# LayerNorm statistics of two batches in one instruction, over interleaved elements

## The reference

```
def layernorm(x):                       # no scale, no shift
    return (x - mean(x)) / sqrt(var(x) + 1e-5)

# layer 1: cross attention, 16 heads of 16 features, context of 128 x 128 x 256
q      = layernorm(x) @ Wq + bq
k, v   = split(ctx @ Wkv + bkv)
scores = q k^T / 4
attn   = softmax(scores, axis=query)    # over the queries, not the keys
x1     = x + (attn v) @ Wo + bo

# layer 2: a router picks 96 of 128 tokens of each batch
y      = layernorm(x1)
keep   = top_k(y @ w_router, 96)
out    = x1 + where(keep, gelu(y @ w_block), y)
```

## Time and profile before

| | |
|---|---|
| median of 3 runs | 921.36 us (921.07 to 921.6) |
| the profiled execution, span from first to last instruction | 919.4 us |
| around the span, median minus span | 2.0 us |
| PE, ACT, DVE, POOL busy | 889.4, 879.5, 873.5, 796.8 us |
| DVE: statistics of layer 1 (L746), of layer 2 (L735) | 128 x 411 ns, 128 x 414 ns |
| DVE: aggregation of layer 1 (L751), of layer 2 (L740) | 128 x 173 ns, 128 x 160 ns |
| granted clock of PE over the span | 0.994 of full speed |

### The profile page before, as it was taken

How to read it: one execution, slowest core, us unless ns; L and a number is a source line. 1 busy time by engine, 2 the same in 40 slices (tenths; PEclk the granted TensorE clock), 3 DMA queues, 4 the chain that set the end, 5 groups by cost and what they waited for, 6 DMA issues and landing times. The chain is left out here.

```text
span 919.4 us, 31003 instructions
## 1 busy us (share of the span) xinstructions
PE 889.4 (97%) x10306; PEld 753.9 (82%) x10306; DVE 873.5 (95%) x2320; ACT 879.5 (96%) x4503; POOL 796.8 (87%) x1488
## 2 busy tenths in 40 slices
PE   7899999999999999999999999999999999999973
PEld 6788888888888888888888888888888888888861
DVE  6899999999999999999999999999999999999887
ACT  5999999999999999999999999999999999999983
POOL 4568789999989999899999999999899999998865
PEclk9999999999999999999999999999999999999997
DMA  6222123223223223223223223223223222221102
GB/s 198 62 65 71 46 61 95 57 84 93 57 84 95 60 83 92 58 86 91 70 75 91 59 86 91 71 74 89 76 71 89 76 71 87 76 61 53 49 24 92
DMA packets 70976, 70.45 MB, mean 77 GB/s; under 512 B 12064, under 2 KB 62752, under 8 KB 70816
## 3 DMA queue, kind: packets, MB, share of 16 engines
q1 hardware_dynamic: 69456, 67.68, 25.5%
q10 hardware_dynamic: 1360, 0.79, 0.3%
HBM read 35.13 MB, written 16.78 MB: 56 GB/s over the span
## 5 line engine op out<-in xcount | busy, mean ns | idle before, releaser
L567 ACT ACTIVATE e_sb<-ps_s,neg_max 128x128 f32<-128x128 f32 x2048 | 719.1, 411 | 4.4 <-DVE neg_max L712 3.9
L567 ACT ACTIVATION_READ_ACCUMULATOR e_sb<-ps_s,neg_max 128x1 f32 x2048 | 513.5, 251 | 0.0
L712 DVE TENSOR_REDUCE neg_max<-ps_s 128x4 f32<-128x512 f32 x512 | 329.0, 663 | 26.4 <-PE ps_s L337 26.4
L337 PE MATMUL ps_s<-q_eo,k_sb 32*128 32x256 f32 x2048 | 146.6, 400 | 1.1 <-DVE k_sb L790 0.5
L402 PE MATMUL ps_a<-e_sb,v_pad 128*32 128x128 f32 x4096 | 138.4, 276 | 2.2 <-DVE x_sb L729 1.6
L299 PE MATMUL ps_a<-w_o_sb,o_sb 128*128 128x256 f32 x512 | 133.2, 382 | 2.0 <-DVE v_sb L803 1.9
L299 PE MATMUL ps_t<-w_z_sb,xt_sb 128*128 128x258 f32 x512 | 132.6, 381 | 1.3 <-DVE z_sb L815 1.3
L1042 POOL TENSOR_TENSOR v_pad<-v_sb,recip 128x256 f32<-128x256 f32 x128 | 79.6, 622 | 54.0 <-DVE recip L757 52.5
L402 PEld LDWEIGHTS ps_a<-e_sb,v_pad 128*32 128x32 f32 x4096 | 104.1, 109 | 24.0 <-issue 21.6
L337 PEld LDWEIGHTS ps_s<-q_eo,k_sb 32*128 32x128 f32 x2048 | 92.5, 184 | 29.4 <-ACT e_sb L567 17.0
L1031 POOL TENSOR_TENSOR x_sb<-x_sb,bo_sb 128x256 f32<-128x256 f32 x128 | 114.0, 892 | 0.2
(11 more groups left out here) (102 smaller groups left out, 2197.6 us busy)
## 6 DMA issues: line engine op xcount, KB each, us to landing
x_sb<-in_x SPq DMA_DIRECT2D x64, 256.0 KB, 2.9
c_sb<-in_ctx SPq DMA_DIRECT2D x64, 256.0 KB, 3.1
out<-z_sb SPq DMA_DIRECT2D x64, 256.0 KB, 2.4
q_eo<-q_raw SPq DMA_DIRECT2D x504, 32.0 KB, 2.0
z_sb<-in_L_xattn_Wkv ACTq DMA_DIRECT2D x2, 256.0 KB, 7.2
z_sb<-in_L_xattn_Wq ACTq DMA_DIRECT2D x1, 256.0 KB, 4.5
w_z_sb<-in_L_ffn_w_block SPq DMA_DIRECT2D x1, 256.0 KB, 7.6
w_o_sb<-in_L_xattn_Wo SPq DMA_DIRECT2D x1, 256.0 KB, 7.0
```

The source lines that it names most:

```text
L337: mm = nc.tensor.matmul(ps_s[:, bank(b, j), c, :, :], k_sb[rows, r2, c, h * T:(h + 1) * T], q_eo[rows, r2, :, c, h, :], start=True, stop=True)
L567: last = nc.scalar.activation(e_sb[:, b % 4, j, c, par, :], ps_s[:, bank(b, j), c, par, :], ACT.Exp, bias=neg_max[:, b % 4, h:h + 1], accu ...
L712: nc.vector.tensor_reduce(neg_max[:, b % 4, :].rearrange("p (c j q) -> p j c q", c=C, j=J)[:, j, :, :], ps_s[:, bank(b, j), :, :, :], AX.X ...
```

## The change

Two rows of `x_sb` (or `x1_sb`) that lie 256 elements apart are read by one `bn_stats` as 512 elements, the first element of one batch, the first of the other, the second of one, and so on. The even places are then one batch and the odd places the other, so the six numbers that come out are count, mean and sum of squares of either batch, and no aggregation is needed. The epsilon step on POOL multiplies the sum of squares by 1/256 and adds epsilon in the same instruction. The calls go to every second step: the pair of layer 1 to the start of the odd steps, two steps earlier than the aggregation of its second batch stood before; the pair of layer 2 to the end of the odd steps. The last two batches keep statistics and aggregation of their own in layer 2.

```diff
-        st1 = sb("st1", [P, 4, 6])
-        mv1 = sb("mv1", [P, R, 2])
+        st1 = sb("st1", [P, R // 2, 6])
...
+        count_mean_m2 = "p g (q k) -> p (g q) k"
+        mean1 = st1[:, :, :].rearrange(count_mean_m2, q=2)[:, :, 1]
+        m2_1 = st1[:, :, :].rearrange(count_mean_m2, q=2)[:, :, 2]
...
-            def stats2(b):
-                if has(b):
-                    dve.wait_ge(x1_ready, upto(b))
-                    nc.vector.bn_stats(st2[:, b % 4, :], x1_sb[:, b % R, :]).then_inc(st2_ready, 1)
...
+            def stats2_of_pair(b):
+
+                if b % 2 == 0 and has(b):
+                    dve.wait_ge(x1_ready, upto(b + 1))
+                    nc.vector.bn_stats(st2[:, pair(b), :],
+                                       x1_sb[:, b % R:b % R + 2, :].rearrange("p q e -> p e q")).then_inc(st2_ready, 2)
...
-            def aggregate1(b):
-                if has(b):
-                    dve.wait_ge(st1_ready, upto(b))
-                    nc.vector.bn_aggr(mv1[:, b % R, :], st1[:, b % 4, :]).then_inc(mv1_ready, 1)
...
+            def stats1_of_pair(b):
+
+                if b % 2 == 0 and has(b):
+                    dve.wait_ge(x_in[pair(b)], landed(b))
+                    nc.vector.bn_stats(st1[:, pair(b), :],
+                                       x_sb[:, b % R:b % R + 2, :].rearrange("p q e -> p e q")).then_inc(st1_ready, 2)
...
                 if s >= 4:
-                    stats1(s + 10)
-                aggregate2(s - 3)
+                    stats1_of_pair(s + 10 if s == 4 else s + 11)
...
-                stats2(s - 2)
+                stats2_of_pair(s - 3)
...
-            stats2(B - 2)
-            aggregate2(B - 2)
+            stats2_of_one(B - 2)
+            aggregate2_of_one(B - 2)
...
-                    pool.wait_ge(mv1_ready, upto(b + 1))
-                    nc.gpsimd.tensor_tensor(ve1[:, r], mv1[:, r, 1], eps_sb[:, :], ALU.add).then_inc(ve1_ready, 2)
-                    nc.gpsimd.tensor_scalar(neg_m1[:, r], mv1[:, r, 0], -1.0, None, ALU.mult)
+                    pool.wait_ge(st1_ready, upto(b + 1))
+                    nc.gpsimd.tensor_scalar(ve1[:, r], m2_1[:, r], 1.0 / E, EPS, ALU.mult, ALU.add).then_inc(ve1_ready, 2)
+                    nc.gpsimd.tensor_scalar(neg_m1[:, r], mean1[:, r], -1.0, None, ALU.mult)
```

More of the change, by code:

```diff
@@ L81, in cross_attention_routed_ffn @@
         minus_mean = sb("minus_mean", [P, P])
-        eps_sb = sb("eps_sb", [P, 2])
         minus_half = sb("minus_half", [P, 2])
@@ L90, in cross_attention_routed_ffn @@
         rstd1 = sb("rstd1", [P, R])
-        st2 = sb("st2", [P, 4, 6])
-        mv2 = sb("mv2", [P, R, 2])
+        st2 = sb("st2", [P, R // 2, 6])
+        st2_one = sb("st2_one", [P, 2, 6])
         ve2 = sb("ve2", [P, R])
@@ L104, in cross_attention_routed_ffn @@
         beta = sb("beta", [P, 2, GROUP])
+        count_mean_m2 = "p g (q k) -> p (g q) k"
+        mean1 = st1[:, :, :].rearrange(count_mean_m2, q=2)[:, :, 1]
+        m2_1 = st1[:, :, :].rearrange(count_mean_m2, q=2)[:, :, 2]
+        mean2 = st2[:, :, :].rearrange(count_mean_m2, q=2)[:, :, 1]
+        m2_2 = st2[:, :, :].rearrange(count_mean_m2, q=2)[:, :, 2]
+        mean_var_one = st2[:, :, :].rearrange(count_mean_m2, q=2)[:, :, 1:3]
         raw = z_sb[:, :, :].rearrange("p b e -> p (b e)")
@@ L157, in cross_attention_routed_ffn @@
         w_mean_mm, w_z_ready = sem("w_mean_mm"), sem("w_z_ready")
-        st1_ready, mv1_ready, ve1_ready, rstd1_ready = sem("st1_r"), sem("mv1_r"), sem("ve1_r"), sem("rstd1_r")
-        st2_ready, mv2_ready, ve2_ready, rstd2_ready = sem("st2_r"), sem("mv2_r"), sem("ve2_r"), sem("rstd2_r")
+        st1_ready, ve1_ready, rstd1_ready = sem("st1_r"), sem("ve1_r"), sem("rstd1_r")
+        st2_ready, ve2_ready, rstd2_ready = sem("st2_r"), sem("ve2_r"), sem("rstd2_r")
+        st2_one_ready, mean_var_one_ready = sem("st2_one_r"), sem("mean_var_one_r")
         xhat_ready = sem("xhat_ready")
@@ L730, in residual, with stats2_of_one, aggregate2_of_one @@
                                             ALU.add).then_inc(x1_ready, 1)
-            def stats2(b):
-                if has(b):
-                    dve.wait_ge(x1_ready, upto(b))
-                    nc.vector.bn_stats(st2[:, b % 4, :], x1_sb[:, b % R, :]).then_inc(st2_ready, 1)
-            def aggregate2(b):
-                if has(b):
[L739 to L746, removed]
-            def aggregate1(b):
-                if has(b):
-                    dve.wait_ge(st1_ready, upto(b))
-                    nc.vector.bn_aggr(mv1[:, b % R, :], st1[:, b % 4, :]).then_inc(mv1_ready, 1)
+            def stats2_of_pair(b):
[3 more added lines that the diff above has]
+                                       x1_sb[:, b % R:b % R + 2, :].rearrange("p q e -> p e q")).then_inc(st2_ready, 2)
+            def stats2_of_one(b):
+                dve.wait_ge(x1_ready, upto(b))
+                nc.vector.bn_stats(st2_one[:, b % 2, :], x1_sb[:, b % R, :]).then_inc(st2_one_ready, 1)
+            def aggregate2_of_one(b):
+                dve.wait_ge(st2_one_ready, b - (B - 2) + 1)
+                nc.vector.bn_aggr(mean_var_one[:, b % R, :], st2_one[:, b % 2, :]).then_inc(mean_var_one_ready, 1)
+            def stats1_of_pair(b):
[3 more added lines that the diff above has]
+                                       x_sb[:, b % R:b % R + 2, :].rearrange("p q e -> p e q")).then_inc(st1_ready, 2)
             def inverse_sums(b):
@@ L871, in _ @@
             even_odd_mask()
-            for b in range(2):
-                stats1(b)
-                aggregate1(b)
+            stats1_of_pair(0)
             weights_low("q")
-            for b in range(2, 4):
-                stats1(b)
-                aggregate1(b)
+            stats1_of_pair(2)
             weights_low("k")
@@ L882, in _ @@
             query_bias()
-            for b in range(4, 6):
-                stats1(b)
-                aggregate1(b)
+            stats1_of_pair(4)
             inputs_low(2)
@@ L894, in _ @@
             inputs_low(4)
-            for b in range(6, 8):
-                stats1(b)
-                aggregate1(b)
+            stats1_of_pair(6)
             keys(2)
@@ L907, in _ @@
             inputs_low(6)
-            for b in range(8, 10):
-                stats1(b)
-                aggregate1(b)
+            stats1_of_pair(8)
             queries(4)
@@ L922, in _ @@
                 router(s - 16, 8)
-                if s >= 4:
-                    aggregate1(s + 10)
                 maxima(s, 3)
@@ L944, in _ @@
                 final(s - 16, sure)
-                stats2(s - 2)
+                stats2_of_pair(s - 3)
                 product_scaled(s - 4, sure)
                 if s < 4:
-                    for b in range(2 * s + 6, 2 * s + 8):
-                        stats1(b)
-                        aggregate1(b)
+                    stats1_of_pair(2 * s + 6)
             router(B - 16, 8)
             x1_transposed(B - 4)
-            aggregate2(B - 3)
             router(B - 16, 9)
@@ L968, in _ @@
             residual(B - 1)
-            stats2(B - 1)
-            aggregate2(B - 1)
+            stats2_of_one(B - 1)
+            aggregate2_of_one(B - 1)
             product_scaled(B - 3)
@@ L995, in _ @@
             nc.gpsimd.memset(ident[:, :], 0.0).then_inc(mask_step, 1)
-            nc.gpsimd.memset(eps_sb[:, :], EPS).then_inc(mask_step, 1)
             nc.gpsimd.memset(minus_half[:, :], -0.5).then_inc(mask_step, 1)
@@ L999, in _ @@
             nc.gpsimd.memset(minus_mean[:, :], -1.0 / E).then_inc(mask_step, 1)
-            pool.wait_ge(mask_step, 5)
+            pool.wait_ge(mask_step, 4)
             nc.gpsimd.affine_select(out=ident[:, :], in_=ident[:, :], compare_op=ALU.not_equal, fill=1.0, base=0,
@@ L1051, in rstd2_of_pair @@
                     r = slice(b % R, b % R + 2)
-                    pool.wait_ge(mv2_ready, upto(b + 1))
-                    nc.gpsimd.tensor_tensor(ve2[:, r], mv2[:, r, 1], eps_sb[:, :], ALU.add).then_inc(ve2_ready, 2)
+                    pool.wait_ge(st2_ready, upto(b + 1))
+                    nc.gpsimd.tensor_scalar(ve2[:, r], m2_2[:, r], 1.0 / E, EPS, ALU.mult, ALU.add).then_inc(ve2_ready, 2)
                     pool.wait_ge(ve2_ready, upto(b + 1))
@@ L1057, in rstd2_of_one @@
             def rstd2_of_one(b):
-                pool.wait_ge(mv2_ready, upto(b))
-                nc.gpsimd.tensor_tensor(ve2[:, b % R:b % R + 1], mv2[:, b % R:b % R + 1, 1], eps_sb[:, 0:1], ALU.add).then_inc(ve2_ready, 1)
+                pool.wait_ge(mean_var_one_ready, b - (B - 2) + 1)
+                nc.gpsimd.tensor_scalar(ve2[:, b % R:b % R + 1], m2_2[:, b % R:b % R + 1], 1.0, EPS,
+                                        ALU.mult, ALU.add).then_inc(ve2_ready, 1)
                 pool.wait_ge(ve2_ready, upto(b))
```

2 lines of the change are left out of this document (1 added, 1 removed).

## The result

The changed kernel takes 924.02 us (median of 6 runs, 922.81 to 926.28) against 921.16 us (920.96 to 921.6) for the kernel before on the same chip: a ratio of 1.0032 with an interval of [1.002, 1.0044], slower by 0.3%. 919.8 was forecast. The time lies inside the range, on the wrong side of the kernel before.

The account below looks back on a forecast made before the run. The prediction took PE to bound the steady part, with DVE's lateness costing it 1.6 us in all. Terms of -1.5 - 0.25 + 0.18 = -1.6 gave 919.4 - 1.6 + 2.0 = 919.8 us, range 918.2 to 925.0.

Parts of the forecast that it names:

- The step that failed: Odd steps, layer 1 statistics read earlier against an unchanged x load: claimed cost nothing, with 0.2 us of cover.
- Rival 2: Layer 1 statistics in odd steps: the x load comes too late, losing the loop's gain, 921.2 us; chance 0.12 together with Rival 3.
- Statistics in the loop: DVE's pair statistics: 0.24 us less per step removes PE's pause once in eight steps, gain 1.5 us (1.2 to 1.6).
- Rival 1: Both pair statistics of odd steps: the 1 KB hop per element is paid, 923.2 us at 1055 ns; chance 0.25.
- Rival 3: PE's pause: ACT's copy is late for another reason, relief does not reach PE, 921.2 us; chance 0.12 together with Rival 2.
- Rival 4: Loop: more than PE's pause is won, as an always early DVE also frees buffers early, 918.0 us; chance 0.13.
- Start: Before the first scores: POOL's chain starts earlier after one statistics instruction, -0.25 us taken between 0 and -0.46.
- End: After the last maxima, where DVE leads: pair statistics add 0.26 us, a dropped aggregation saves 0.08, together +0.18.
- The sum: Whole kernel: loop, start and end terms, -1.5 - 0.25 + 0.18 = -1.6 us.

Follow-up runs that it names:

- e1: Changed kernel with layer 1 pair statistics taken two steps later, still at the start of odd steps: 919.79 us, ratio 0.999 to the kernel before.
- e2: Changed kernel with SP issuing the x load ahead of the queries' rearrangements and the store, DVE unchanged: 919.63 us, ratio 0.999 to the kernel before.
- e5: Changed kernel with layer 1 pair statistics one step later, at the start of even steps: 921.29 us, ratio 1.0003 to the kernel before.
- e4: e1 with the 512 elements read side by side instead of in turn, which changes the output: 919.78 us, ratio 0.9987 to the kernel before.

## Why the prediction was wrong

**The step that failed** is "Layer 1 is now read two steps earlier, against a load that is issued as before. ... Cost nothing, with 0.2 us of cover." The cover was read from one step, 59, and from the median landing, 2.9. The issue itself wanders by over a microsecond from pair to pair, in the rows of before too, so the median step's cover is not that of the late ones. Landings add to it. In the loop of the kernel before none took more than 3.3 us (the 9.0 of the earlier trace rows belongs to the start); in the changed kernel 44 of 50 took 2.7 to 3.2 and six 3.5 to 4.3, four of these right before steps 43, 67, 77 and 103, among the latest of all. The prediction also took the issue as given. It is not: SP issues the load behind the queries of the same odd step, so the late statistics delay the next load, and there are spells of late steps (39, 41, 43; 67, 69, 71; 77, 79). Measured, this term is +5.3 us: 717.07 in the changed kernel against 711.80 in e1 and 711.87 in e2, from step 16 to step 120. That the reading moved by "two steps" is right for the second batch of a pair only; the wait for the load, which the first batch had, moved by one, and e5, which moves it back by this one step, has no wait.

**Rival 2** named the mechanism, and its sign in the profile was right ("layer 1 statistics wait for x loads in many steps": 31 of them). Its price was capped without reason: "the odd steps pay again what the loop gained" sets the loss equal to a gain with which it has nothing to do. The lateness of 1.07 on DVE, 0.77 past the 0.30 that the rival itself allowed, made PE's step 77 alone 7.42 - 6.78 = 0.64 us longer.

**Statistics in the loop** (-1.5, 1.2 to 1.6): right, and a little small. With the wait taken away (e1, e2) a round falls from 54.90 to 54.75, 13 times 0.15 = 2.0 us, more than the 1.6 that the prediction took for all that can be won there: in e1 the step in which the router's round begins, 60, is shorter as well, 6.88 instead of 6.93. DVE is 0.20 late in step 61 of e1 (maxima 1.49 after the scores), 0.16 was forecast. DVE's busy time fell by 22.6 us and not by 31: the instruction holds the engine for 0.63 (the one at 546.73, to the next start) and not 0.60, which is 0.21 less per step, 27 us; the 512 reductions are 4 ns longer each, 2 us; the last 2 to 3 us were not traced.

**Rival 1**, the paid hop, is out: 692 against 680 ns (e4). Two of its figures were off besides: 1055 ns is three quarters of the way between its ends and not midway, and 922.6 for 1019 ns does not follow from its terms (0.86 us in eight steps, less than the 1.05 of cover, leaves only the end, some 0.5). The Trainium skill has both sides of it. Vector Engine (DVE) Microarchitecture Reference, section 5.2, reports a one-source operation that alternates between two distant regions at the full rate, and this agrees; its 1.73 ns a column for a hop on every element, an estimated 1019 ns, and the penalty of Advanced Engine Details and Errata, section Memory Cachelines, do not show here.

**Rival 3** is out: the pause went with DVE's lateness. **Rival 4** has little for it: e1 and e2 end at 919.8 and 919.6.

**Start** (-0.25): nothing. POOL's chain did begin earlier, and its second operation was held as long, as the timeline of POOL shows:

```profile
5.29 0.19 POOL L1002 TENSOR_SCALAR ve<-st 128x2 f32<-128x2 f32 x1 [2.72 <-DVE st L759]
5.57 0.61 POOL L1003 TENSOR_SCALAR neg_m<-st 128x2 f32<-128x2 f32 x1
6.15 0.71 POOL L1005 TENSOR_TENSOR rstd<-ve,minus_half 128x2 f32<-128x2 f32 x1
6.97 1.61 POOL L1014 TENSOR_SCALAR xhat<-x_sb,neg_m,rstd 128x256 f32<-128x256 f32 x2
```

The 0.61 lies beside DVE's weight subtraction, 5.40 to 6.09; the same operation took 0.22 before. From the start of the first statistics, the power begins 1.75 us after it instead of 1.96, so 0.21 was still won there. The two normalisations behind it lose it again: 1.61 us, where POOL's timeline of before has

```profile
7.65 1.10 POOL L1022 TENSOR_SCALAR xhat<-x_sb,neg_m,rstd 128x256 f32<-128x256 f32 x2
```

The first scores come 10.61 after the first statistics instead of 10.53. Why the normalisations took longer was not tested.

**End** (+0.18): from the end of the last maxima to the end of the keep row 3.50 us instead of 3.30, +0.20. What was not foreseen is some -0.37 behind it, below.

**The sum** without the failed step, -1.6, came out as -1.1 (e1) and -1.3 (e2) in the medians: 919.79 and 919.63 against 920.93. That is less than the 2.0 of the rounds, and that e1 meets the forecast of 919.8 is in part luck, since the loop gave more than its term and the start nothing; the profiled execution of e1, at 918.91, is the fastest of its 11. Both are some 0.1% faster than the kernel before, by an interval that ends at 0.9999, and their intervals lie clear of the changed kernel's, which begins at 1.002.

## What to carry to other kernels

Before a reader is moved ahead, take the distance between issue and need over all steps, its worst and not its median, and follow what stands in the queue before the issue: if the reader's own result is among it, a late read delays the next one, and the price can exceed what one step's lateness suggests. When an engine's work shrinks and the kernel slows, look for a wait that is not on an engine; the busy share of the engine that bounds may not move at all. Of a change that saves work and moves it, the saving can be kept and the move undone: here that is one index (e1) or one line of SP's loop (e2).

## What was not expected of the hardware

- `bn_stats` over 512 elements that alternate 1 KB apart takes 692 ns, over 512 that lie together 680; over 256 it is 411 to 414.
- The eight rearrangements of 32 KB occupy SP's queue for 4.94 to 6.25 us before and after, 0.6 to 0.8 each, and a store or a load of 256 KB mostly 0.47 to 0.59. A DMA's place in this queue was worth more here than its transfer time.
- DVE and POOL seem to hold each other up where their operations lie side by side: the 0.61 above is one case. At the end of the kernel before, DVE's product of a batch with its GELU factor (L821) took 0.89 us (at 896.59 of its timeline, beside POOL's product of 0.62), in the changed kernel 0.52; that fits the -0.37 at the end. It was not tested by itself and stays a reading.
